# A new order inside the attention unit: the output projection moved to mid-unit, routing logits moved to another bank, the maxima written in place

## What is computed

```python
h = layernorm(x) * (1 + ca) + sa
x = x + ga * attention(h)      # 16 heads of 16, rotary positions, causal softmax
h = layernorm(x) * (1 + cb) + sb
x = x + gb * experts(h)        # each row goes to the one of 8 experts with the largest logit
```

## Time and profile before

| | us |
|---|---|
| median of three runs | 781.2 |
| profiled execution | 779.62 |
| its span, first to last instruction | 777.9 |
| attention: set-up, up to the first exponential | 65.2 |
| attention: 32 units | 430.5 |
| attention: last tiles | 23.2 |
| routed part | 259.0 |

### The profile page before, as it was taken

One profiled execution on the slowest core, in us unless ns is written; L12 is line 12 of the kernel. 1 busy time (PEld: TensorE's weight loads), 2 busy tenths in 40 slices (PEclk: granted clock), 3 DMA queues, 4 the chain that ended last, 5 costly groups with the idle time before them and its releaser, 6 DMA issues. The chain is left out here.

```text
span 777.9 us, 21258 instructions
## 1 busy us (share of the span) xinstructions
PE 672.6 (86%) x7438; PEld 424.9 (55%) x7438; DVE 588.5 (76%) x1215; ACT 521.0 (67%) x1061; POOL 478.9 (62%) x635
## 2 busy tenths in 40 slices
PE   5766888899999999999999888765999999999993
PEld 4432444445454544545445443444787878788772
DVE  6567888888888988888888767348577777777774
ACT  2334889899989989989899888642444444444441
POOL 4422566788878888888988777832245454535331
PEclk9797999999999999999999999956999999999997
DMA  8102423335444443634424446349566651323000
GB/s 266 38 8 49 124 89 103 102 107 146 123 139 136 140 140 109 162 111 133 137 86 153 120 146 149 121 149 369 193 214 197 215 167 59 90 83 91 31 20 0
DMA packets 61364, 97.49 MB, mean 125 GB/s; under 512 B 8405, under 2 KB 42318, under 8 KB 60753
## 3 DMA queue, kind: packets, MB, share of 16 engines
q1 hardware_dynamic: 56272, 79.36, 33.3%
q0 software_dynamic: 4992, 16.79, 6.8%
HBM read 69.47 MB, written 34.51 MB: 134 GB/s over the span
## 5 line engine op out<-in xcount | busy, mean ns | idle before, releaser
L1165 DVE TENSOR_REDUCE row_max<-ps_max 128x2 f32<-128x768 f32 (+2 forms) x192 | 200.0, 1042 | 39.5 <-PE ps_max L676 39.4
L959 ACT ACTIVATE prob<-ps_sc 128x1024 f32<-128x1024 f32 (+1 forms) x192 | 169.7, 884 | 45.9 <-PE ps_sc L703 45.3
L1515 PE MATMUL ps_h<-tok_t,w_all 128*128 128x128 f16 x1872 | 156.1, 219 | 0.7 <-DVE tok_t L1690 0.5
L1515 PEld LDWEIGHTS ps_h<-tok_t,w_all 128*128 x1872 | 130.8, 98 | 41.7 <-issue 2.2
L1585 ACT ACTIVATE hid<-ps_h,b_t 128x128 f32<-128x128 f32 x312 | 88.9, 368 | 96.1 <-PE ps_h L1515 96.1
L1432 POOL DMA_INDIRECT slot_mem<-row_dram,token x39 | 55.6, 1426 | 120.4 <-DVE y L1725 100.5
L445 POOL TENSOR_SCALAR_AFFINE_SELECT prob<-prob 128x512 f32<-128x512 f32 x128 | 86.1, 672 | 60.7 <-ACT prob L959 59.8
L1528 PE MATMUL ps_y<-w_all,hid_parts 128*128 x312 | 118.0, 379 | 1.9 <-DVE hid_parts L1700 1.6
L669 PE MATMUL ps_max<-k_t,q_t 64*128 64x512 f16 (+3 forms) x512 | 68.8, 305 | 35.6 <-DVE row_max L1165 35.1
L716 PE MATMUL ps_pv<-prob,v_sb 128*32 128x512 f32 (+3 forms) x1024 | 88.8, 442 | 0.3
L1530 PE MATMUL ps_y<-w_all,hid_parts 128*128 x312 | 85.0, 273 | 0.0
(11 more groups left out here) (269 smaller groups left out, 1362.9 us busy)
## 6 DMA issues: line engine op xcount, KB each, us to landing
raw<-w SPq DMA_DIRECT2D x64, 256.0 KB, 3.0
w_dram<-halves SPq DMA_DIRECT2D x64, 256.0 KB, 3.3
w_all<-w_dram SPq DMA_DIRECT2D x20, 512.0 KB, 4.8
row_dram<-rows SPq DMA_DIRECT2D x32, 256.0 KB, 3.4
w_all<-w_dram SPq DMA_DIRECT2D x3, 2048.0 KB, 13.5
mod_rows<-mods_dram SPq DMA_DIRECT2D x16, 256.0 KB, 7.1
row_dram<-mods_dram SPq DMA_DIRECT2D x32, 128.0 KB, 4.8
xs<-x SPq DMA_DIRECT2D x24, 128.0 KB, 3.2
```

The source lines that it names most:

```text
L959: nc.scalar.activation(p_kb[:, :, first * L:(first + n) * L], ps_sc[:, :, 0:n * L], ACT.Exp, scale=SCALE).then_inc(exp_done, 1)
L1165: nc.vector.tensor_reduce(dst, ps_max[:, :, 0:n * L].rearrange("p j (m l) -> p j m l", m=n), AX.X, ALU.max).then_inc(max_done, 1)
L1515: last = mm(o, w[:, :, k, f, :][:, bass.ds(e, 1), :].rearrange("p e m -> p (e m)"), tok_t[:, j % 2, piece, k, :], start=(n == 0 and f % HF ...
```

## The change

- **Maxima written in place.** `maxima` writes straight into the float16 column of `q_aug`. The buffer `row_max`, the instruction `negated` and its semaphore go; the constant column of `k_aug` is -1 in place of 1. `shift_rows` waits for the sixth maxima themselves.
- **Output projection a unit later, mid-unit.** `project_out(X - 1)` stands behind `tokens_first` in shot 2 and writes to `ps_b`, after `rope` has read it; the transposes of Q, which write `ps_b` next, wait for the residual. `residual(X - 1)` follows `divide` directly, both behind the third maxima; `row_statistics` follows the fourth maxima. The last unit also projects tile X in shot 5.
- **Logits in `ps_a`.** They are made in shots 4 and 5, where Z % 4 = 3 (U % 4 = 2), after the values in `ps_a` have been read; `keep_logit_t` stands before exponential 5 and `keep_logits` behind it. The transposes of K wait for them.
- **Bias first.** The bias product of Q and K is issued in shot 0.
- **ACT.** The scaling instruction (L969) becomes `scaled_piece`; that of the unit's second piece comes behind `keep_shift`.
- **POOL.** New order: `low_piece(2U - 1)`, `low_h`, `row_modulate(U - 6)`, `add_const`, mask 0, `rotate`, `rstd_of`, mask 1, `low_piece(2U)`, `gate_weights`, mask 2, `row_power`, mask 3, `row_hat`.

```diff
-            nc.gpsimd.memset(k_aug[...][:, :, 3 * DK:3 * DK + 1], 1.0).then_inc(consts_done, 1)
+            nc.gpsimd.memset(k_aug[...][:, :, 3 * DK:3 * DK + 1], -1.0).then_inc(consts_done, 1)
...
# POOL, unit loop
+                T, Y = U + LEAD, U - QT - 1
+                if U:
+                    low_piece(2 * U - 1)
+                if U and T < NT:
+                    low_h(T)
+                if Y > 0:
+                    row_modulate(Y - 1)
                 if U >= QT - 1:
                     add_const(U - QT + 1)
                 clear_future(U, 0)
-                if U % QT >= QT - KC:
-                    gate_weights(U // QT, U % QT - QT + KC)
...
                 low_piece(2 * U)
+                if U % QT >= QT - KC:
+                    gate_weights(U // QT, U % QT - QT + KC)
                 clear_future(U, 2)
+                if Y >= 0:
+                    row_power(Y)
                 clear_future(U, 3)
-                low_piece(2 * U + 1)
-                if U >= QT + 1:
-                    row_power(U - QT - 1)
-                    row_hat(U - QT - 1)
-                if T + 1 < NT:
-                    low_h(T + 1)
-                if U >= QT + 1:
-                    row_modulate(U - QT - 1)
+                if Y >= 0:
+                    row_hat(Y)
...
# PE
             def shift_rows(V):
-                pe.wait_ge(negmax_done, V + 1)
+                pe.wait_ge(max_done, NSHOT * V + NSHOT)
...
+                    if s == 0:
+                        if U:
+                            weigh(U - 1, 2)
+                            weigh(U - 1, 3)
+                        if T < NT:
+                            project_bias(ps_b[:, :], T)
+                    if s == 1:
+                        if T < NT:
+                            for part in range(2):
+                                project_qk(T, part, ps_b[:, :])
+                        if Z >= 0:
+                            ge(pe, att_kept, X)
+                            h_transposes(Z, ps_nd)
                     if s == 2:
                         if T < NT:
                             project_v(T, ps_a[:, :], T)
                         ge(pe, htr_kept, Z + 1)
+                        ge(pe, att_kept, X)
                         if U:
                             tokens_first(U - 1)
+                        if X > 0:
+                            if T < NT:
+                                pe.wait_ge(rope_done, 3 * T + 3)
+                            project_out(X - 1, ps_b[:, :])
...
                         weigh(U, 1)
+                        if Z >= 0 and Z % QT == QT - 1:
+                            if T < NT:
+                                pe.wait_ge(v_kept, T + 1)
+                            logit_products(Z // QT, ps_a)
                     if s == 5:
-                        if X >= 0:
-                            project_out(X, ps_nd)
+                        if Z >= 0 and Z % QT == QT - 1:
+                            logit_transposes(Z // QT, ps_a)
+                        if U == NU - 1:
+                            pe.wait_ge(x1_done, X)
+                            project_out(X, ps_b[:, :])
                         if T < NT:
+                            ge(pe, x1_done, X)
                             q_transposes(T, ps_b[:, :])
                         if V < NU:
                             shift_rows(V)
                         if T < NT:
+                            if Z >= 0:
+                                ge(pe, logits_kept, (Z + 1) // QT)
                             k_transposes(T, ps_a[:, :])
...
# ACT
                     if s == 2:
                         high_piece(2 * U)
+                        scaled_piece(2 * U)
...
+                    if s == 4 and Z >= 0 and Z % QT == QT - 1:
+                        keep_logit_t(Z // QT, ps_a)
+                if Z >= 0 and Z % QT == QT - 1:
+                    keep_logits(Z // QT, ps_a)
                 high_piece(2 * U + 1)
                 if V < NU:
                     keep_shift(V)
+                scaled_piece(2 * U + 1)
...
# DVE
                     if V < NU:
                         maxima(V, s)
-                    if s == 0 and X > 0:
-                        residual(X - 1, ps_nd)
-                    if s == 1 and T + 1 < NT:
+                    if s == 0 and T + 1 < NT:
                         statistics(T + 1)
                     if s == 1 and T < NT:
                         rope(T, ps_b[:, :])
-                    if s == 3 and U:
+                    if s == 2 and U:
                         divide(U - 1)
+                    if s == 2 and X > 0:
+                        residual(X - 1, ps_b)
+                    if s == 3 and X > 0:
+                        row_statistics(X - 1)
                     if s == 4 and T < NT:
                         lo_parts(T)
-                if V < NU:
-                    negated(V)
                 if T < NT:
                     keep_qt(T, ps_b[:, :])
-                if X > 0:
-                    row_statistics(X - 1)
                 if T + 1 < NT:
                     modulate(T + 1, ps_nd)
```

More of the change, by code:

```diff
@@ L538, in _ @@
                 low_piece(2 * U)
+                if U % QT >= QT - KC:
+                    gate_weights(U // QT, U % QT - QT + KC)
                 clear_future(U, 2)
+                if Y >= 0:
+                    row_power(Y)
                 clear_future(U, 3)
-                if U == NU - 1:
-                    for X in range(NT - QT + 1, NT):
-                        add_const(X)
-                low_piece(2 * U + 1)
-                if U >= QT + 1:
-                    row_power(U - QT - 1)
-                    row_hat(U - QT - 1)
-                if T + 1 < NT:
-                    low_h(T + 1)
-                if U >= QT + 1:
-                    row_modulate(U - QT - 1)
+                if Y >= 0:
+                    row_hat(Y)
+            for X in range(NT - QT + 1, NT):
+                add_const(X)
+            low_piece(2 * NU - 1)
+            row_modulate(NT - QT - 2)
             first = NT - QT
@@ L613, in x_transposes, with project_bias, project_qk @@
                 last.then_inc(xt_ps, 1)
-            def project_qk(T, part, ps, kept_before):
+            def project_bias(ps, kept_before):
+                ge(pe, qt_kept, kept_before)
+                mm(ps, ones3[:, :], bias3[:, 0:2 * D], start=True, stop=False)
+            def project_qk(T, part, ps):
                 if part == 0:
                     pe.wait_ge(h_high, T + 1)
-                    ge(pe, qt_kept, kept_before)
-                    mm(ps, ones3[:, :], bias3[:, 0:2 * D], start=True, stop=False)
                     for k in range(KC):
@@ L779, in _ @@
                 ps_q, ps_v = lead_banks(T)
+                project_bias(ps_q, T - 1)
                 for part in range(2):
-                    project_qk(T, part, ps_q, T - 1)
+                    project_qk(T, part, ps_q)
                 project_v(T, ps_v, T - 1)
@@ L819, in _ @@
                     scores(U, s)
[L820 to L825, removed]
-                    if s == 1 and T < NT:
-                        for part in range(2):
-                            project_qk(T, part, ps_b[:, :], T)
-                    if s == 1 and Z > 0 and Z % QT == 0:
-                        logit_transposes(Z // QT - 1, ps_nd)
-                    if Z >= 0 and s == h_shot(Z):
-                        ge(pe, logits_kept, Z // QT)
-                        pe.wait_ge(x1_done, X)
-                        h_transposes(Z, ps_nd)
+                    if s == 0:
[11 more added lines that the diff above has]
+                            h_transposes(Z, ps_nd)
                     if s == 2:
@@ L1008, in _ @@
                         keep_u(U - 1)
-                    if s == 1 and Z > 0 and Z % QT == 0:
-                        keep_logit_t(Z // QT - 1, ps_nd)
-                        keep_logits(Z // QT - 1, ps_nd)
-                    if Z >= 0 and s == h_shot(Z):
+                    if s == 1 and Z >= 0:
                         keep_h(Z, ps_nd)
@@ L1163, in maxima @@
                 dve.wait_ge(max_ps, NSHOT * V + s + 1)
[L1164 removed]
+                par, g = place(V)
+                column = q_aug[:, par, qt, :].rearrange("p (h w) -> p h w", w=HW)[:, HG * g:HG * (g + 1), 3 * DK]
+                dst = column.rearrange("p (m j) -> p j m", j=2)[:, :, first:first + n]
                 nc.vector.tensor_reduce(dst, ps_max[:, :, 0:n * L].rearrange("p j (m l) -> p j m l", m=n),
                                         AX.X, ALU.max).then_inc(max_done, 1)
[L1168 to L1173 removed]
             def divide(W):
@@ L1283, in _ @@
             first = NT - QT
-            residual(first - 1, ps_nd)
+            residual(first - 1, ps_b)
             row_statistics(first - 1)
```

24 lines of the change are left out of this document (7 added, 17 removed).

## The result

The changed kernel takes 771.3 us (median of 4 runs, 769.0 to 771.9) against 781.0 for the kernel before, run beside it: a ratio of 0.9865 [0.9838, 0.9893]. A second measurement of the same kernel, with more runs, gave 772.05 us (770.78 to 773.07), 0.989 [0.9872, 0.9908]. The forecast was 776.0. The kernel became faster by about twice what was forecast; the time lies in the range.

What follows compares the result with a forecast made beforehand. No engine fills the attention units; a chain of maxima and PE blocks, then PE's own order, bounds them. Terms sum to -3.9 from the profiled 779.6, 775.7, given as 776.0; range 765 to 784.

Steps and rivals of the forecast that it cites:

- The chain: In each attention unit: maxima, PE block, maxima, and at the end PE's own order, set the unit's length.
- Projection mid-unit: Shot 2 of an ordinary unit: project_out at 5.22, fourth block 0.20 later, residual at 6.48, fourth maxima at 6.84.
- the five units that now hold the logits: Units 10, 14, 18, 22, 26: 14.0 each, logits costing 0.1 beyond the blocked lo_parts; +1.5 in all.
- The forecast's last line: End of the sum: -3.9 gives 775.7; the runs' median is 1.6 above the profiled execution, so 776.0 was given.
- The price of the collision: Mask 2 meets lo_parts in ordinary units: second instruction 0.42 longer, on the chain, making the unit 13.73; bounds 0 and 0.64.
- the rival in which the second instruction goes ahead of the mask: lo_parts' second instruction escapes mask 2: ordinary units 13.31, total 771.8; chance 0.25.
- The whole mask ahead: All of mask 2 precedes lo_parts' second instruction: 0.64 in place of 0.42 per ordinary unit, 778.2; chance 0.12.
- free gating units: Units with gate_weights also escape the lo_parts collision: 11 units x 0.6 less, 765.2; chance 0.12.
- POOL as the bound: Late row_hat delays low_h in gating units, so PE stands at project_qk: +8.8, 784.8; chance 0.15.
- Unit 0 and units 1 and 4: First units, where the negation's wait was hardly covered: unit 0 -1.2, units 1 and 4 -0.7 each.
- Unit 27: No Q and K projections covered the logits there, and PE waited 1.52 and 0.81: -2.3.
- Unit 31: Last unit trades logits for a second projection; POOL's order behind the loop has the same work: 0.

Runs made afterwards that it cites:

- Experiment 1: Changed kernel, with GpSimd waiting for lo_parts to finish before it starts mask 2: 761.15 us, 0.9762; ordinary units 13.10.
- 9: Changed kernel, with the output projection one block later, behind the scores of shot 3, and its residual behind the fourth maxima: 776.8 us, 0.9934.
- 10: Changed kernel, with only the bias product back in shot 1, behind the wait for the high half of h: 776.2 us, 0.9925.
- experiment 3: Changed kernel, with the maxima in their own buffer and the negating instruction behind the sixth maxima again: 785.5 us, 1.007.

## Why the prediction was right, and where it was wrong

**The chain: right but for its last link.** Forecast and trace have the same links: the scores of shot 2 at 3.70, project_out, the residual, the fourth to sixth maxima without a gap, lo_parts caught in the second instruction, then PE's order. Experiments 1, 9 and 10 moved three of the links, and the unit moved with each.

**The step that failed: two start-to-start distances in "Projection mid-unit".** First, "Tokens at 3.70 + 0.92 = 4.62 and 0.60 long; project_out at 5.22" took a matmul row's length for the distance to what follows. It is 0.44: project_out starts at 5.07. The earlier trace rows had shown it, since the transposes of Q, 0.61 long, are followed by L686 after 0.44. Second, "the residual can start 1.26 after the projection's start" came from unit 31, where the projection's row is 1.13 long; in mid-unit it is 1.03 long and the distance is 1.16. Together 0.25, and the starts behind them keep that lead: fourth maxima 0.27 earlier than forecast, lo_parts 0.29. Of it 0.22 is left at shift_rows (11.46 against 11.68). From the start of lo_parts to the end of the sixth maxima it is 1.81, where the forecast has 0.66 + 0.42 + 0.68 = 1.76, and shift_rows start 0.08 behind that end, directly behind the transposes of Q. These wait for lo_parts too (0.79), a link that the forecast left out, and it ends almost together with the forecast's. The way from there to the next exponential is 2.00 against 2.05. So an ordinary unit takes 13.46, not 13.73. Ten of them make 2.2 of the 4.4 us that were missed; the five units that now hold the logits make another 0.9 (13.78 against 14.0). The forecast's last line does not follow from its sum either: 775.7 and the 1.6 of the median make 777.3, not 776.0, so by its own terms the forecast gain was 3.9 us.

**The price of the collision: right.** Mask 2 comes 3.11 behind exponential 3 (forecast 3.10), and the second instruction is 0.43 longer (0.42). That the two met at all was closer than forecast: with lo_parts 0.29 early and exponential 3 only 0.13, the mask comes 0.22 behind lo_parts in place of 0.05, and the second instruction starts at 0.34. The Trainium skill, "SBUF — State Buffer", section "Who interferes with whom", would have the later of the two blocked for the whole of the earlier, thus 0.64. The trace again shows less than that, 0.43 for a mask of 0.70.

**Rivals.** The time, 771.3, is that of the rival in which the second instruction goes ahead of the mask (771.8), but its mechanism is not there: that instruction takes 0.85 in every ordinary unit after. Experiment 1 shows what it would have given with the true distances, 13.10 in place of the 13.31 that the prediction had. The whole mask ahead, free gating units and POOL as the bound are not seen either; gating units take 13.78 where 13.9 was forecast, with the first instruction of lo_parts at 0.73 or 0.74 and the second at 0.85.

**Single terms.** Unit 0 and units 1 and 4 came out as forecast. Unit 27 gave 1.6 in place of 2.3: PE no longer waits for logits, but ACT still stands up to 1.15 there for scores. Unit 31 was costed at 0 and gave 0.7. The trace of before shows why, in its row of TensorE for the logits' transposes and the tokens there:

```profile
489.54 0.33 PE L768 MATMUL ps_nd<-ident,logit_t 128*128 128x128 f32 x1 [0.71 <-ACT logit_t L941]
...
491.32 0.66 PE L730 MATMUL ps_nd<-ident,u_sb 128*128 128x128 f32 x4 [0.72 <-ACT h_tr L937]
```

The logits and their waits lay inside the unit; the second projection that takes their place comes behind the last scores.

**What the parts are worth, and what the change left lying.** Undone one at a time in the new order, the maxima in place are worth 13.5 us, the logits 9 and the scaling 8 (both with some clock in them), the bias product 4 to 5; the projection in mid-unit costs 7. These do not add up to the gain, and a part's worth depends on the order around it: the maxima in place alone give no measurable gain in the old order. That the projection's place costs 7 us is the collision in other words, for with the mask held both places take the same in an ordinary unit, and 760 to 762 us in all. The changed kernel with that one wait takes 761.2 us, 2.4% less than before.

**Open.** What the logits' place and the wait of keep_v would give back in the gating units was not tried. Why units 27 to 31 had a lower clock in some of the runs was not settled.

## What to carry to other kernels

Work out chains from the distances between starts of neighbouring rows, never from a row's length, and take a distance from a stretch with the same neighbours: a quarter of a microsecond in each of ten repeated units was half of the error here. Work that moves off one engine's path may have been the cover of a collision elsewhere, as the projection was here, so look at what the freed engine will wait for next and hold the colliding work back if it has slack; one wait of GpSimd was worth as much as the whole change. An edit costed in one order says nothing of its worth in another: removing the negation gave nothing measurable in the old order and 13.5 us in the new.

## What the runs showed of the hardware that had not been expected

Of two VectorE instructions that follow each other directly, here it is the second that pays when GpSimd's mask arrives during the first. The second instruction of lo_parts, over 32 tiles (busy us, mean ns of one), after and in experiment 1:

```profile
L1174 DVE TENSOR_TENSOR k_aug<-rot,k_aug 128x256 f16<-128x256 f32 x32 | 23.8, 744 | 0.0
```

```profile
L1176 DVE TENSOR_TENSOR k_aug<-rot,k_aug 128x256 f16<-128x256 f32 x32 | 13.3, 416 | 0.0
```

So the mask costs the second instruction 0.33 on average and 0.43 in an ordinary unit. The rows read as if the mask were served between the two: it takes 0.70 in unit 12, hardly more than its usual 0.64. Even an instruction on 128x16 elements is held. The negation takes 400 ns on average in experiment 3, where it falls beside mask 3, and 0.20 us in unit 12 of the kernel before, where no mask lies beside it:

```profile
L1195 DVE TENSOR_SCALAR q_aug<-row_max 128x16 f16<-128x16 f32 x32 | 12.8, 400 | 1.1
```

```profile
243.06 0.20 DVE L1172 TENSOR_SCALAR q_aug<-row_max 128x16 f16<-128x16 f32 x1
```

And short idle stretches of PE, 0.48 of 1.5 us and 0.55 of 2.0 us busy, were followed by some 3 us at 1.2 GHz in two of the experiments, while in the changed kernel a stretch with 0.53 of 1.5 us busy (433.0 to 434.5) was followed by the full clock.
